# The last FFN of a four-layer stack with its inner index taken in steps of 8, and its weights loaded three tiles earlier

## The reference, cut to what matters

```
def mx_quant(x):                    # blocks of 32 along the contraction axis share an exponent
    xb = x.reshape(..., n // 32, 32)
    scale = 2 ** (floor(log2(max|xb|)) - 6)
    return clip(round(xb / scale), -128, 127) * scale
h = mx_layernorm(x, ln_w, ln_b)                      # 256 channels
h = mx_quant(h) @ mx_quant(W1).T + b1                # 256 -> 1024
h = gelu(h)                                          # rounded to bf16
h = mx_quant(h) @ mx_quant(W2).T + b2                # 1024 -> 256
out = x + h
```

## Time and profile before

| | |
|---|---|
| median of 3 runs | 616.39 us |
| the profiled execution's own time | 620.55 us |
| its span | 618.5 us |
| TensorE matmul busy | 376.3 us (61%) |
| VectorE busy | 429.3 us (69%) |
| ScalarE busy | 229.8 us (37%) |
| GpSimd busy | 180.1 us (29%) |
| mean granted TensorE clock | 0.83 of full speed |

### The profile page before, as it was taken

The page is one execution under the profiler, slowest core; times in us unless marked ns, Lnnn a source line. Parts: engine busy times, 40 slices in busy tenths (PEclk is TensorE's granted clock), DMA queues, the critical chain, the costliest instruction groups (busy, mean ns, idle before and its releaser), DMA issues.

```text
span 618.5 us, 5497 instructions
## 1 busy us (share of the span) xinstructions
PE 376.3 (61%) x1680; PEld 259.5 (42%) x1680; DVE 429.3 (69%) x615; ACT 229.8 (37%) x333; POOL 180.1 (29%) x116
## 2 busy tenths in 40 slices
PE   0000260435454204999999999946948699798552
PEld 0000220213243102667767766624646577676421
DVE  5999759798774886856966867326673346789873
ACT  4626651447756121222222222202202236365451
POOL 4600213953003483440360330036364600000000
PEclk9999856575678555899999999987977699799875
DMA  8900000000027521281061561995001300000000
GB/s 296 333 0 0 1 0 0 1 0 0 0 98 246 210 76 47 91 302 38 27 205 35 196 212 34 45 153 179 17 10 51 93 1 0 1 10 17 10 17 17
DMA packets 34673, 47.46 MB, mean 77 GB/s; under 512 B 5699, under 2 KB 28758, under 8 KB 34646
## 3 DMA queue, kind: packets, MB, share of 16 engines
q1 hardware_dynamic: 23046, 31.76, 15.1%
q10 hardware_dynamic: 10032, 11.14, 8.2%
q0 software_dynamic: 1568, 4.20, 2.1%
HBM read 37.67 MB, written 9.44 MB: 76 GB/s over the span
## 4 chain that ended last, share of the span: by engine, by line
PE 42%; DVE 19%; issue 19%; POOL 7%; ACT 6%; DMA 6%; ACTq 1%; SPq 0%; POOLq 0%; DVEq 0%
PE bank L1259 12%; PE bank L1243 11%; PE bank L1309 6%; DMA ekv<-in_w3b 4%; POOL slot_rows L375 3%; PE bank L1269 3%; PE bank L1163 3%; DVE scr L723 2%; DVE small L1065 1%; PE bank L1283 1%; DMA small<-in_s_gu 1%; DVE scr L973 1%; POOL ekv L326 1%; PE bank L1318 1%; POOL scr L334 1%
## 5 line engine op out<-in xcount | busy, mean ns | idle before, releaser
L1243 PE MATMUL bank<-big,yT 128*128 x384 | 91.6, 394 | 16.8 <-ACT yT L587 16.8
L1259 PE MATMUL bank<-big,ygT 128*128 x192 | 90.5, 616 | 1.8 <-ACT ygT L544 1.1
L1243 PEld LDWEIGHTS bank<-big,yT 128*128 128x128 f32 x384 | 74.3, 198 | 28.3 <-issue 18.4
L954 DVE TENSOR_TENSOR yT<-bank,big 128x512 f32<-128x512 f32 x48 | 32.8, 689 | 42.7 <-PE bank L1259 42.7
L351 POOL TENSOR_TENSOR small<-small 128x2 f32<-128x2 f32 (+1 forms) x9 | 9.1, 1009 | 173.4 <-DVE small L1032 88.0
L587 ACT ACTIVATE yT<-bank 128x512 f32<-128x512 f32 x24 | 14.3, 597 | 109.3 <-DVE yo L226 82.7
L1259 PEld LDWEIGHTS bank<-big,ygT 128*128 128x128 f32 x192 | 36.0, 198 | 39.3 <-issue 39.3
L1309 PE MATMUL bank<-yT,scr 128*128 128x256 f32 x192 | 46.7, 403 | 0.0
L1163 PE MATMUL bank<-big 128*128 128x512 bf16 x64 | 22.6, 515 | 30.9 <-DVE big L828 29.9
L1309 PEld LDWEIGHTS bank<-yT,scr 128*128 128x128 f32 x192 | 38.6, 205 | 5.5
L340 POOL TENSOR_TENSOR scr<-scr 128x1024 f32<-128x1024 f32 x5 | 15.5, 3108 | 87.1 <-DVE scr L723 87.1
(11 more groups left out here) (284 smaller groups left out, 891.7 us busy)
## 6 DMA issues: line engine op xcount, KB each, us to landing
big<-in_moe_w SPq DMA_DIRECT2D x16, 1024.0 KB, 7.0
big<-in_moe_b SPq DMA_DIRECT2D x8, 512.0 KB, 8.8
slot_rows<-zeros SPq DMA_DIRECT2D x1, 3072.0 KB, 12.9
xg<-slot_rows ACTq DMA_DIRECT2D x24, 128.0 KB, 2.1
slot_outputs<-yo ACTq DMA_DIRECT2D x24, 128.0 KB, 1.7
v<-in_kT SPq DMA_DIRECT2D x1, 1024.0 KB, 5.0
yT<-in_xT SPq DMA_DIRECT2D x1, 1024.0 KB, 8.1
big<-in_gateT SPq DMA_DIRECT2D x1, 1024.0 KB, 10.1
```

The source lines that it names most:

```text
L954: ve.tensor_tensor(h1[:, h * 512:(h + 1) * 512], ps[1 + 2 * (j % 2) + h][:], big[:, bass.ds(at + (B1_AT + h * 512), 512)], ALU.add).then_i ...
L1243: ins = te.matmul(ps[7][:, 0:C], hT[:, c], big[:, bass.ds(at + (W2_AT + c * C), C)], start=(c == 0), stop=(c == IC - 1))
L1259: ins = te.matmul(ps[1 + 2 * (j % 2) + h][:], ygT[:, j % 2, k], big[:, bass.ds(at + (k * HI + h * 512), 512)], start=(k == 0), stop=(k == ...
```

## The change

The inner index is now h = 8i + r, stored at position 128r + i. W1's rows 8p to 8p+7 lie in partition p, so that one partition is one contiguous piece of 8 KB. b1 and W2 stay in their natural order, and TensorE reads them with a step of 8 elements. A block of 32 is then four neighbours i in each of the eight r.

- W1 and W2 are issued by ScalarE ahead of tile 15 instead of 18, two transfers instead of five. The wait for the last ratio gives way to waits for the last scan and the last product with `v`.
- The rows (`s_down`, `ln_w`, `ln_b`, and now b1 and b2, all broadcast to 128 partitions) are issued at tile 18, after the wait for the last ratio; layer 2's weights at tile 19.
- SP's six bias loads and GpSimd's zeroing of `brf` are gone. GpSimd waits for the five rows instead; so does VectorE at tile 23.
- GpSimd's rounding of each weight ends in one subtraction over 2048 elements, in natural order, instead of two halves.
- `gelu_scales` takes its maximum over an access pattern of 32 blocks, 8 r, 4 i, and writes `inverse` and `unit` 128 elements wide. `gelu_quant` broadcasts these over r.

```
-            pe.wait_ge(s["w3q"], 2 * KC)
+            pe.wait_ge(s["w3q"], 2)
-                        src = w3q[:, 1, k * H3 + c * P:k * H3 + (c + 1) * P]
+                        src = w3q[:, 1, k * H3:(k + 1) * H3].rearrange("p (i r) -> p r i", r=HC3)[:, c]

-            sp.wait_ge(s["br_zero"], 1)
-            for row in (0, 64, 96):
-                sp.dma_start(brf[row:row + 1, 0:H3].rearrange("p (j n) -> p j n", n=32),
-                             A["b3a"].rearrange("(n j) -> j n", n=32).unsqueeze(0), ...)
-                sp.dma_start(brf[row:row + 1, H3:H3 + C], A["b3b"].unsqueeze(0)).then_inc(s["ld_bias"], 16)

-            pool.wait_ge(s["ratio_ready"], 2 * L)
-            gp.memset(brf, 0.0).then_inc(s["br_zero"], 1)
-            pool.wait_ge(s["ld_bias"], 16 * 6)
+            pool.wait_ge(s["ld_l3rows"], 16 * 5)
...
-                for k in range(KC):
-                    n = slice(32 * k, 32 * (k + 1))
-                    turned = w3q[:, m, k * H3:(k + 1) * H3].rearrange("p (j n) -> p n j", n=32) if m else \
-                        w3q[:, m, k * H3:(k + 1) * H3].rearrange("p (n j) -> p n j", j=32)
-                    gp.tensor_tensor(turned, w3v[:, n], half[:, n], ALU.subtract).then_inc(s["w3q"], 1)
+                gp.tensor_tensor(w3q[:, m].rearrange("p (n j) -> p n j", j=32), w3v, half, ALU.subtract).then_inc(s["w3q"], 1)

             def load_w3():
-                act.wait_ge(s["ratio_ready"], 2 * L)
-                rows = A["w3a"].rearrange("(n c j) k -> j n c k", n=32, c=HC3)
-                for j in range(4):
-                    act.dma_start(w3nat[0][32 * j:32 * (j + 1)].rearrange("p (c k) -> p c k", c=HC3), rows[j]).then_inc(s["ld_w3"], 16)
+                act.wait_ge(s["scanned"], 2 * len(POOL_SUMS))
+                act.wait_ge(s["gv_ready"], 2 * L)
+                act.dma_start(w3nat[0].rearrange("p (c k) -> p c k", c=HC3),
+                              A["w3a"].rearrange("(p c) k -> p c k", c=HC3)).then_inc(s["ld_w3"], 16)

             def load_rows():
-                for dst, n in ((sdrow, "s_down"), (lnw, "ln_w"), (lnb, "ln_b")):
+                act.wait_ge(s["ratio_ready"], 2 * L)
+                for dst, n in ((sdrow, "s_down"), (lnw, "ln_w"), (lnb, "ln_b"), (brf[:, 0:H3], "b3a"), (brf[:, H3:H3 + C], "b3b")):

             for j in range(TILES):
-                if j == 18:
+                if j == 15:
                     load_w3()
+                elif j == 18:
+                    load_rows()
                 elif j == 19:
-                    load_rows()
-                elif j == 20:
                     load_l2()

-                link(ve.tensor_reduce(top3, gl3[i % 2].rearrange("p (j n) -> p n j", n=32), AX.X, ALU.max, ...))
+                link(ve.tensor_reduce(top3, gl3[i % 2].rearrange("p (r n q) -> p n r q", r=HC3, q=4), AX.XY, ALU.max, ...))
...
+                bits = top3.bitcast(I32).unsqueeze(2).to_broadcast(by_block)   # by_block = [P, 32, 4]
...
-                    te.matmul(ps[4 + h][:], pick[:], br[:, h * 512:(h + 1) * 512], start=False, stop=True).then_inc(s["u3_ready"], 1)
+                    te.matmul(ps[4 + h][:], pick[:], br[:, 0:H3].rearrange("p (i r) -> p r i", r=HC3)[:, 4 * h:4 * h + 4], start=False, stop=True).then_inc(s["u3_ready"], 1)
```

More of the change, by code:

```diff
@@ L196, in bass_adaln_ffn_stack @@
             r3_tr r3_copy sig3 y3_ready var3 pow3 hq3 hq3_tr hq3T u3_ready a3_ready g3_ready q3_ready
-            q3_tr q3T_ready d3_ready ob_ready x_done stored w3_copy2 r3_copy2 bias_added br_zero ld_bias br_ready""".split()
+            q3_tr q3T_ready d3_ready ob_ready x_done stored w3_copy2 r3_copy2 bias_added br_ready""".split()
         s = {n: sem(n) for n in NAMES}
@@ L279, in _ @@
                 sp.wait_ge(s["ld_w"], 48 * (e + 1))
-            sp.wait_ge(s["br_zero"], 1)
-            for row in (0, 64, 96):
-                sp.dma_start(brf[row:row + 1, 0:H3].rearrange("p (j n) -> p j n", n=32),
-                             A["b3a"].rearrange("(n j) -> j n", n=32).unsqueeze(0),
-                             allow_slow_non_contiguous=True).then_inc(s["ld_bias"], 16)
-                sp.dma_start(brf[row:row + 1, H3:H3 + C], A["b3b"].unsqueeze(0)).then_inc(s["ld_bias"], 16)
             out_v = out.rearrange("b (s p) c -> p (b s) c", p=P)
@@ L961, in _ @@
                     if j == 19:
-                        dve.wait_ge(s["ld_w3"], 80)
+                        dve.wait_ge(s["ld_w3"], 32)
                     if j % 2:
@@ L971, in _ @@
                     ve.tensor_scalar(qgu, qgu.bitcast(I32), 128.0, None, ALU.subtract)
-                    dve.wait_ge(s["ld_l3rows"], 16 * 3)
+                    dve.wait_ge(s["ld_l3rows"], 16 * 5)
                     ve.scalar_tensor_tensor(qd, qd.bitcast(I32), 128.0, sdrow.unsqueeze(1).to_broadcast([P, HC2, C]),
@@ L1057, in norm_quant @@
                 dve.wait_ge(s["hq3"], p + 1)
-            unit = ex3[:, 1].bitcast(BF16)[:, 0:32]
-            inverse = ex3[:, 2].bitcast(BF16)[:, 0:32]
+            unit = ex3[:, 1:3].rearrange("p m n -> p (m n)").bitcast(BF16)[:, 0:P]
+            inverse = ex3[:, 1:3].rearrange("p m n -> p (m n)").bitcast(BF16)[:, P:2 * P]
+            by_block = [P, 32, 4]
             def gelu_scales(i):
@@ L1064, in gelu_scales @@
                 top3 = ex3[:, 0, 0:32]
-                link(ve.tensor_reduce(top3, gl3[i % 2].rearrange("p (j n) -> p n j", n=32), AX.X, ALU.max, apply_absolute_value=True))
+                link(ve.tensor_reduce(top3, gl3[i % 2].rearrange("p (r n q) -> p n r q", r=HC3, q=4), AX.XY, ALU.max, apply_absolute_value=True))
                 link(ve.tensor_scalar(top3.bitcast(I32), top3.bitcast(I32), 0x7F800000, None, ALU.bitwise_and))
                 link(ve.tensor_scalar(top3, top3, 2.0 ** -120, None, ALU.max))
-                ve.tensor_scalar(inverse.bitcast(I16), top3.bitcast(I32), -1.0 / 65536, 260.0 * 128, ALU.mult, ALU.add)
-                link(ve.tensor_scalar(unit.bitcast(I16), top3.bitcast(I32), 1.0 / 65536, -6.0 * 128, ALU.mult, ALU.add))
+                bits = top3.bitcast(I32).unsqueeze(2).to_broadcast(by_block)
+                ve.tensor_scalar(inverse.bitcast(I16).rearrange("p (n q) -> p n q", q=4), bits, -1.0 / 65536, 260.0 * 128, ALU.mult, ALU.add)
+                link(ve.tensor_scalar(unit.bitcast(I16).rearrange("p (n q) -> p n q", q=4), bits, 1.0 / 65536, -6.0 * 128, ALU.mult, ALU.add))
             def gelu_quant(i):
-                by_block = [P, 32, 32]
                 t = m3[:, 0:512].bitcast(BF16)
-                g3 = gl3[i % 2].rearrange("p (j n) -> p j n", n=32)
-                link(ve.tensor_tensor(t.rearrange("p (j n) -> p j n", n=32), g3, inverse.unsqueeze(1).to_broadcast(by_block), ALU.mult))
+                t3 = t.rearrange("p (r i) -> p r i", r=HC3)
+                g3 = gl3[i % 2].rearrange("p (r i) -> p r i", r=HC3)
+                link(ve.tensor_tensor(t3, g3, inverse.unsqueeze(1).to_broadcast([P, HC3, P]), ALU.mult))
                 link(ve.tensor_scalar(t, t, MAGIC, MAGIC, ALU.add, ALU.subtract))
@@ L1079, in gelu_quant @@
                     dve.wait_ge(s["q3_tr"], i - 1)
-                ve.tensor_tensor(q3[i % 2].rearrange("p (j n) -> p j n", n=32), t.rearrange("p (j n) -> p j n", n=32),
-                                 unit.unsqueeze(1).to_broadcast(by_block), ALU.mult).then_inc(s["q3_ready"], 1)
+                ve.tensor_tensor(q3[i % 2].rearrange("p (r i) -> p r i", r=HC3), t3,
+                                 unit.unsqueeze(1).to_broadcast([P, HC3, P]), ALU.mult).then_inc(s["q3_ready"], 1)
                 dve.wait_ge(s["q3_ready"], i + 1)
```

## The result

| | before | after |
|---|---|---|
| median (4 runs each) | 617.11 us | 599.46 us |
| ratio, 95% interval | | 0.9714 [0.968, 0.9747] |
| the profiled execution's time, its span | 620.55, 618.5 us | 599.17, 597.4 us |
| mean granted TensorE clock | 0.83 | 0.863 |
| TensorE matmul busy | 376.3 us | 379.5 us |

The forecast was 593.4 us in a range of 587 to 600. The time is inside, close to the upper end: the gain is 17.65 us instead of 23.0. Ratios are given as recorded, beside the medians; they are not exactly quotients of medians, and where the two tell a different size both stand. TensorE is busier than before by 3.2 us although it does the same work, and that is the clue to what is missing.

The account below looks back on a forecast made before the run. It took TensorE to bound the expert tiles, except for waits on W2's slow DMA and at tile 23. Terms -16.2 (loads and tile 19) - 4.8 - 0.8 - 2.0 + 0.8 = -23.0, from 616.39 to 593.4 us; range 587 to 600.

Parts of the forecast that it names:

- the loads, -16.5: Expert tiles 18 to 22: with W1 and W2 loaded from tile 15, the 16.5 us lost waiting for W2 go.
- tile 23, -4.8: Tile 23: GpSimd's unturned subtraction for W2 ends sooner, so VectorE's conversions end at 454.1 instead of 458.9; -4.8 us.
- the maximum, -2.0: Last FFN: the maximum's runs of four save 0.6 us, net 0.4 after small steps, five times; -2.0 us.
- tile 19, +0.3: Tile 19: GpSimd's five bias steps run beside VectorE's small steps and delay its copy; +0.3 us, at worst 1.5.
- the clock, -0.8: Tile 23's second product: less TensorE idleness beforehand makes the 16 matmuls faster; -0.8 us, between 0 and 3.1.
- the step of 16 bytes, +0.8: Last FFN's bias matmuls: TensorE's strided reading costs a factor of 1.6 on six in the chain; +0.8 us.
- Rival C: Last FFN: all 16 bias matmuls double and their ScalarE readers wait; +3.5 instead of +0.8, 596.1 us; chance 0.10.
- rival A: Tile 23: the wait stays, GpSimd still overlapping VectorE's conversions or TensorE coming later; -17.4, 599.0 us; chance 0.18.
- B: Tile 18: the load of `xg`, queued behind 2 MB on ScalarE, comes 5.4 us late; 598.8 us; chance 0.08.
- D: Last FFN: the maximum's four-dimensional pattern makes it slow, so the kernel is slower than before; 636 at 10 us each; chance 0.02.
- E: Expert tiles: the DMA is slow for another reason than b1 and the tiles still wait; about 612 us; chance 0.05.

Follow-up runs that it names:

- the first of these experiments: The changed kernel with the bias of the last FFN's first product read contiguously by TensorE, so added in the wrong order: 593.33 us, ratio 0.9557.
- the run with the other steps: The changed kernel with TensorE reading the last FFN's biases at steps of 4 and 8 bytes (up projection's halves) and 32 bytes (down projection): 597.68 us.

## Why the prediction came out as it did

**Right: the loads, -16.5.** With b1 alone in one piece six tiles took 16.5 us less; the whole run was 14.4 us shorter by the medians and 16.3 by the ratio, whose interval leaves 12.9 to 19.7. The reading of the earlier trace rows, that b1's single elements clog the engines, was said to be my reading only; now it is shown, by 8.1 against 22 us of landing. The part played by the early issue was left open in the forecast. It is nothing. And with single elements still there, issuing early only moves the stall to the issuing queue.

**Right: tile 23, -4.8.** The gap fell by 5.01 us, and came back with the turned writing (7.96). The mechanism is that of the rows: VectorE's conversion ends after GpSimd's instruction does. The Trainium skill (SBUF — State Buffer, "Who interferes with whom") has the two engines share a pair of ports; the trace agrees at two places: 2.64 against 0.20 us for 64 elements beside GpSimd, 5.69 against 1.75 us for the second conversion.

**Too small: the maximum, -2.0.** One execution went from 1.88 to 1.22, -0.66 where -0.6 was taken, and the two small steps cost 0.05 us more each, not 0.1. Five times -0.56 are -2.8. On the path it is 3.0 to 3.1 us by the run with the old pattern. From the last stretch of the kernel before to that of the changed kernel with b1 read contiguously it is 3.5 (132.5 to 129.0).

**Too small: tile 19, +0.3.** It cost 1.0, since GpSimd's rows end at 407.3 and catch a second step.

**Not repeatable: the clock, -0.8.** The 16 matmuls after a gap of 2.93 us took 5.40 us in the changed kernel's profile and 3.71 in its repetition; after the long gap 6.74 and 5.15 in before's two. The difference within one kernel is larger than the term. The seven profiles with a gap of 2.92 or 2.93 us have 3.71, 3.72, four times 5.40, and 6.71.

**Wrong: the step of 16 bytes, +0.8.** This is the step that failed. The forecast took "the nearest row", VectorE's, "a factor of 1.6", and "six of them are in the chain". The runs show a factor of 4.1 at full clock and 2 at the low one, eight in the chain, and 5.2 us. "From above, twice the time on all: 16 x 0.22 = 3.5" was no bound at all: nothing in the trace limits the factor to two. VectorE's factor of 1.6 was no guide to TensorE's 4.1. Rival C had the mechanism, ScalarE waiting for the bias matmuls, and the size from the same false bound, 3.5 us. The range held by luck in this respect: it reached to 600 for the sake of rival A, while C alone ended at 596.1. The Trainium skill (SBUF — State Buffer, "Door 1") says of a step of 8 bf16 both that it is free and that full rate needs two hits per line of 16 bytes. The trace agrees with neither sentence in full: by that line, one hit costs four times the contiguous reading (0.90 us), two hits twice (0.46), and four hits run at full rate (0.23). At the low clock two hits do run at the contiguous rate (0.44 against 0.43), as the second sentence has it.

**The sum by stretches of the trace.** "Second group" is TensorE's second group of four transposes of `x` (line 1296 before, 1287 after), the start of the second pair of token tiles. Each kernel has two profiles:

| stretch, us | before | changed | change | forecast |
|---|---|---|---|---|
| tile 17 to tile 23 | 64.39, 64.08 | 48.93, 48.93 | -15.46, -15.15 | -16.2 |
| tile 23 to the second group | 41.45, 38.33 | 33.61, 31.82 | -7.84, -6.51 | -5.6 |
| second group to the end | 132.50, 132.49 | 134.13, 134.24 | +1.63, +1.75 | -1.2 |

The first and the last stretch repeat within 0.3 us; the middle one holds the clock's scatter. The forecast had the sign of the last stretch wrong, and that is the step of 16 bytes. With b1 read contiguously, in the first of these experiments, the last stretch is 129.0 us.

The terms as measured: -16.5 + 1.0 - 5.0 - 3.1 + 5.2 = -18.4, and -17.65 were found by the medians; the forecast's -23.0 with the step at 5.2 and tile 19 at 1.0 would have been -17.9. The rest is within the scatter of the medians.

**The other rivals.** A gave 599.0, the number nearest to the result, and is refuted: the wait fell from 7.94 to 2.93 us. A right time shows nothing of a reason. B: no wait for `xg` stands at tile 18, and 2 MB did no harm. D: the pattern with runs of four is faster, not slower. E: it does what it says.

**The base.** The median of 616.39 was of three runs; with a fourth it was 617.11, and beside the three groups of experiments before took 619.79, 619.22 and 620.71. The changed kernel has the same scatter, 599.46 and 601.36. The ratios remove that of the base, but for terms of 2 to 5 us they are no better: they make the step 9.7 us and the maximum nothing. For such terms a stretch of the trace that repeats is the number to keep.

## What to carry to other kernels

When data are laid out anew to spare one engine a turned write, list every reader of the new layout on every engine and price each from a row of that same engine; if there is none, leave the upper bound open or avoid the reader, here by one copy of 2.2 us on an idle engine that saved 5 to 6. Two edits that free the same wait don't add up: each alone took 14 to 15 us off the median, and with b1 in one piece the early issue added nothing. And look at transfers made of single elements first: the slow load was not the load's fault.

## What the hardware showed that was not expected

- TensorE's time for a moving operand of bf16 goes with its step: 4 bytes free, 8 bytes twice, 16 and 32 bytes four times (0.22, 0.46, 0.90 us for 512 columns) at a granted clock of 1.00. The time with a step is the same at the low clock (0.88 us for 16 bytes), where the contiguous reading takes 0.43: there 8 bytes are free and 16 cost twice. Weight loads suffered less: W1's and W2's together, of which W2's have the step of 16 bytes, have a median of 120 ns and a maximum of 155, where before all took 98.
- Transfers of 4-byte elements on one queue slow another queue's 1 MB from 8.1 to 22 us, and hold an issue on ScalarE's queue for 5.45 us, where the changed kernel's same issue takes 0.47.
- GpSimd's subtraction of 2048 elements takes 3.64 us, but 10.83 with the result written turned (3.78 for W1's, in two halves and not turned). Not all of that is the writing: the turned halves take 4.72 and 6.50 us, W1's 1.91 each, and VectorE's first conversion runs during the second half, from the end of the first at 451.7 us to 453.3. Without those 1.6 us the second is 4.9 by my estimate, near the first. A turned half then costs 2.5 times one that is not turned (4.72 against 1.91).
- After one and the same gap of 2.93 us the same 16 matmuls took 3.71 us in one execution of the changed kernel and 5.40 in another, and 6.71 in the run with the other steps.
